# Cross-attention of a perceiver layer: keys and values by seven block products per chunk, key stacks through HBM

## The reference, cut to what matters

```python
# x (1, 256, 512), ctx_1024 (1, 25088, 512); 16 heads of 32
def _L0_xattn_ref(query, key, value, Wq, Wk, Wv, Wo):
    q = (query @ Wq.T).reshape(B, L, H, D) * scale
    k = (key @ Wk.T).reshape(B, -1, H, D)
    v = (value @ Wv.T).reshape(B, -1, H, D)
    scores = jax.nn.sigmoid(jnp.einsum('blhd,bshd->bhls', q, k))
    o = jnp.einsum('bhls,bshd->blhd', scores, v).reshape(B, L, E)
    return o @ Wo.T
x = x + _L0_xattn_ref(_layernorm(x), ctx_1024, ctx_1024, Wq, Wk, Wv, Wo)
x = x + _L0_attn_ref(_layernorm(x), ...)     # causal, 256 rows
x = x + _L0_ffn_ref(_layernorm(x), ...)      # 512 -> 2048 -> 2048 -> 2048 -> 512
```

## Time and profile before

| | |
|---|---|
| median of 3 runs | 2120.26 us (2120.01 to 2121.39) |
| span of the profiled execution | 2119.5 us |
| TensorE busy | 2096.5 us, 99% of the span |
| ScalarE busy | 1361.7 us, 64% |
| VectorE busy | 1190.9 us, 56% |
| GpSimd busy | 1022.3 us, 48% |
| DMA | 157.09 MB, mean 74 GB/s |

### The profile page before, as it was taken

The page is one execution under the profiler, slowest core; times in us unless marked ns, Lnnn a source line. Parts: engine busy times, 40 slices in busy tenths (PEclk is TensorE's granted clock), DMA queues, the critical chain, the costliest instruction groups (busy, mean ns, idle before and its releaser), DMA issues. The chain is left out here.

```text
span 2119.5 us, 42205 instructions
## 1 busy us (share of the span) xinstructions
PE 2096.5 (99%) x15810; PEld 1632.6 (77%) x15812; DVE 1190.9 (56%) x1495; ACT 1361.7 (64%) x1702; POOL 1022.3 (48%) x900
## 2 busy tenths in 40 slices
PE   9999999999999999999999999999999999988999
PEld 6777777777777777777777777777777777746998
DVE  6656556565565665656556565565655656525422
ACT  7666666666666666666666666666666666632764
POOL 5066564665646656466564665646656460000000
PEclk9999999999999999999999999999999999999999
DMA  5111211112111121111211112111121110122774
GB/s 179 42 60 40 74 45 61 58 40 74 45 61 57 40 74 45 62 57 40 74 45 63 56 40 74 45 63 56 40 74 45 63 56 21 65 101 112 277 278 168
DMA packets 43908, 157.09 MB, mean 74 GB/s; under 512 B 5600, under 2 KB 5600, under 8 KB 31200
## 3 DMA queue, kind: packets, MB, share of 16 engines
q1 hardware_dynamic: 43872, 156.59, 20.5%
HBM read 154.47 MB, written 0.52 MB: 73 GB/s over the span
## 5 line engine op out<-in xcount | busy, mean ns | idle before, releaser
L302 ACT ACTIVATE probs<-sc 128x1024 f32<-128x1024 f32 x784 | 761.6, 1022 | 371.5 <-PE sc L463 366.8
L352 DVE TENSOR_TENSOR k_stack<-kp,k_stack 32x512 fp32r<-32x512 f32 x772 | 529.5, 686 | 720.0 <-ACT k_stack L295 701.8
L295 ACT ACTIVATE k_stack<-kp 32x512 fp32r<-32x512 f32 x772 | 456.3, 591 | 257.4 <-PE kp L443 243.2
L267 POOL TENSOR_TENSOR piece_hi<-piece,zero 128x512 fp32r<-128x512 f32 x176 | 220.1, 1251 | 666.6 <-DMA piece<-w_all_dram 642.6
L463 PEld LDWEIGHTS sc<-rows_r,k_stack 96*128 96x128 f32 x3136 | 413.2, 190 | 100.0 <-issue 83.6
L463 PE MATMUL sc<-rows_r,k_stack 96*128 96x256 f32 x3136 | 460.1, 289 | 0.9 <-DMA k_stack<-k_stack 0.9
L454 PE MATMUL vp<-weights_r,c_hi 128*128 128x512 f32 x1568 | 392.9, 392 | 0.0
L443 PE MATMUL kp<-c_hi,weights_r 128*128 128x512 f32 x1544 | 386.8, 392 | 0.0
L474 PE MATMUL acc<-probs,v 128*32 128x256 f32 x6272 | 381.3, 382 | 0.1
L454 PEld LDWEIGHTS vp<-weights_r,c_hi 128*128 128x128 f32 x1568 | 282.0, 189 | 51.2 <-issue 0.8
L443 PEld LDWEIGHTS kp<-c_hi,weights_r 128*128 128x128 f32 x1544 | 277.2, 188 | 49.8
(11 more groups left out here) (135 smaller groups left out, 882.8 us busy)
## 6 DMA issues: line engine op xcount, KB each, us to landing
ctx_raw<-ctxT_dram SPq DMA_DIRECT2D x49, 1024.0 KB, 4.8
piece<-w_all_dram SPq DMA_DIRECT2D x178, 256.0 KB, 4.7
w_raw<-w_all_dram SPq DMA_DIRECT2D x44, 1024.0 KB, 4.8
weights<-wqk_dram SPq DMA_DIRECT2D x2, 1024.0 KB, 6.1
probs<-wqT_dram SPq DMA_DIRECT2D x1, 1024.0 KB, 6.0
probs<-wkT_dram SPq DMA_DIRECT2D x1, 1024.0 KB, 8.0
probs<-wvT_dram SPq DMA_DIRECT2D x1, 1024.0 KB, 11.9
k_stack<-k_stack SPq DMA_DIRECT2D x4, 256.0 KB, 3.0
```

The source lines that it names most:

```text
L267: nc.gpsimd.tensor_tensor(piece_hi[:], piece[:, t % 2, :], zero[:].to_broadcast([P, PIECE]), ALU.add).then_inc(piece_rounded, 1)
L295: nc.scalar.activation(kst[0:D, par, j, g, :], source[D * j:D * (j + 1), :], ACT.Copy).then_inc(k_hi, 1)
L302: nc.scalar.activation(probs[:, t % 2, g, :], sc[g % 2][:], ACT.Sigmoid).then_inc(probs_ready, 1)
L352: nc.vector.tensor_tensor(kst[D:2 * D, par, j, g, :], source[D * j:D * (j + 1), :], f32(kst[0:D, par, j, g, :]), ALU.subtract).then_inc(k_ ...
```

## The change

**Seven products.** The keys of a chunk are a product of a 512 by 512 weight matrix and 512 by 512 numbers of context, and so are the values. Both are now cut into 2 by 2 blocks of 256 and made by Strassen's scheme: seven block products of sums of blocks, in place of eight, with Winograd's order of the sums. A block product has 12 matmuls of 256 columns (two row halves, three terms, two steps of contraction), `k_product` and `v_product`. The seven sums of weight blocks are made once, at the start, and stay in SBUF (`wk`, `wv_c`). The seven sums of context blocks are made for each chunk (`x_combo`), hi and lo, into one set of buffers `xc`, each as soon as the value product of the chunk before it has read the old one. The products are added up in PSUM where the scheme allows it, and elsewhere by VectorE (`k_summed`, `v_summed`) or ScalarE (`k_part`, `k_first`, `v_part`, `v_first`).

**Key stacks through HBM.** A quarter of the keys (128 rows of heads by 256 context rows, two such tiles) comes out with the heads' dimensions in all 128 partitions. Its hi part and its lo part are written to a buffer in HBM (`kept`, "k_rows") and read back from there into the stack: hi rows twice, lo rows once, each time into 32 partitions. That makes 8 stores and 12 loads of 256 KB a chunk, all on SyncE's queue. The queries take the same way once.

**Two tiles weighed in one stretch.** Values are now kept for a whole chunk, twice (`v`), and `weigh` runs for tiles 0 and 1 together and for 2 and 3 together. The last chunk has no projections any more. The scan's four pieces are spread over SyncE's list.

```diff
@@ cross_attention
+        xc = sb("x_combos", [P, 7, 2, 2, HS], F32R)
...
+        kr_hi, kr_lo = sb("k_rows_hi", [P, 2, 2, HS], F32R), sb("k_rows_lo", [P, 2, 2, HS], F32R)
+        v, vt = sb("v", [P, 2, TC, E]), sb("v_part", [P, 2, HE])
@@ block.sync
+            def keep_rows(m, q):
+                at = q % 2
+                sp.wait_ge(k_hi, m * 3 + q)
+                sp.dma_start(kept[q, 0].rearrange("d r j n -> j d r n"), f32(kr_hi[:, at, :, :])).then_inc(hi_kept[q], 16)
+                sp.wait_ge(k_lo, m * 3 + q)
+                sp.dma_start(kept[q, 1].rearrange("d r j n -> j d r n"), f32(kr_lo[:, at, :, :])).then_inc(lo_kept[q], 16)
+            def stack_rows(m, q):
+                i, j = QUADRANT[q]
+                to = f32(kst[:, j, 2 * i:2 * i + 2, :, :])
+                sp.wait_ge(hi_kept[q], m * 16 + 16)
+                sp.dma_start(to[0:D], kept[q, 0]).then_inc(stacked[q], 16)
+                sp.dma_start(to[2 * D:3 * D], kept[q, 0]).then_inc(stacked[q], 16)
+                sp.wait_ge(lo_kept[q], m * 16 + 16)
+                sp.dma_start(to[D:2 * D], kept[q, 1]).then_inc(stacked[q], 16)
...
             def one(c, par, first, k_next, split_next, load_next, looped):
...
+                scan_piece(0)
+                if k_next:
+                    keep_first(m)
+                    scan_piece(1)
+                    sp.wait_ge(scores_ready, c * (TC * G) + (G + 2))
+                    stack_rows(m, 0)
+                    scan_piece(2)
+                    keep_rows(m, 1)
+                    keep_rows(m, 2)
+                    stack_rows(m, 1)
+                    keep_rows(m, 3)
+                    sp.wait_ge(scores_ready, c * (TC * G) + TC * G)
+                    stack_rows(m, 2)
+                if load_next:
+                    sp.wait_ge(x_ready, c * 7 + 14)
+                    sp.dma_start(raw[:], ctxT[c + 3]).then_inc(ctx_loaded, 16)
+                if k_next:
+                    stack_rows(m, 3)
+                scan_piece(3)
@@ block.vector
+            def x_combo(c, i):
+                if i == 1:
+                    dve.wait_ge(ctx_loaded, c * 16 + 32)
+                x_sums(c + 1, i)
+                dve.wait_ge(v_made, c * 7 + (7 + i))
+                nc.vector.tensor_copy(xc[:, i - 1, :, 0, :], x_source(raw, i)).then_inc(x_hi, 1)
+                x_rest(c + 1, i)
...
+                for i in range(1, 8):
+                    if i == 2:
+                        k_first_rest(m)
+                    elif i >= 3:
+                        k_summed(m, i)
+                        v_summed(m, 1 - par, i)
+                    if split_next:
+                        x_combo(c, i)
@@ block.tensor
+            TERMS = ((0, 0), (1, 0), (0, 1))
+            FRESH = (1, 3, 6)
+            def k_product(m, i, first=False):
...
+                elif i == 3:
+                    pe.wait_ge(k11_lo, m + 1)
+                elif i > 3:
+                    pe.wait_ge(k_sum, m * 5 + (i - 3))
+                n = 0
+                for r in range(2):
+                    for a, b in TERMS:
+                        for k in range(2):
+                            last = nc.tensor.matmul(k2[:, r, :], wk[i - 1][:, k, a, r * P:(r + 1) * P],
+                                                    xc[:, i - 1, k, b, :], start=i in FRESH and n == 0, stop=n == 11,
...
```

More of the change, by code:

```diff
@@ L309, in _, with k_part @@
[L309 to L315 removed]
+            def k_part(m):
+                act.wait_ge(k_made, m * 7 + 1)
+                nc.scalar.activation(kc[:, 0, :, :], k2, ACT.Copy).then_inc(kt_saved, 1)
@@ new lines, in v_summed @@
+            def v_summed(m, par, i):
+                add, q = SUMS[i]
+                dve.wait_ge(v_made, m * 7 + i)
+                nc.vector.tensor_tensor(v_at(par, q), vt[:] if add == "t" else v_at(par, add), v2,
+                                        ALU.add).then_inc(v_sum, 1)
+            for i in range(1, 8):
+                if i >= 3:
+                    if i == 3:
+                        dve.wait_ge(x_ready, 1)
+                    x_sums(0, i)
+                wk_rest(i)
+                x_rest(0, i)
+                if i == 2:
+                    dve.wait_ge(q_hi, 1)
+                    nc.vector.scalar_tensor_tensor(out=qr_lo, in0=sc[0][:], scalar=SCALE, in1=f32(qr_hi),
+                                                   op0=ALU.mult, op1=ALU.subtract).then_inc(q_lo, 1)
+                elif i == 4:
+                    k_first_rest(0, first=True)
+                elif i >= 5:
+                    k_summed(0, i - 2, first=True)
+                    v_summed(0, 0, i - 2)
@@ new lines, in _ @@
+            for i in (6, 7):
+                k_summed(0, i, first=True)
+                v_summed(0, 0, i)
+            def one(c, par, first, k_next, split_next, load_next, looped):
+                m = c + 1
+                if not k_next:
+                    return
+                for i in range(1, 8):
+                    if i == 2:
+                        k_first_rest(m)
[4 more added lines that the diff above has]
+                        x_combo(c, i)
@@ new lines, in v_product @@
+            def v_product(m, i, first=False):
+                if i == 1 and not first:
+                    pe.wait_ge(v_sum, m * 5)
+                elif i == 2:
+                    pe.wait_ge(vt_saved, m + 1)
+                elif i == 3:
+                    pe.wait_ge(v11_saved, m + 1)
+                elif i > 3:
+                    pe.wait_ge(v_sum, m * 5 + (i - 3))
+                n = 0
+                for r in range(2):
+                    for a, b in TERMS:
+                        for k in range(2):
+                            last = nc.tensor.matmul(v2[:, r, :], xc[:, i - 1, k, b, r * P:(r + 1) * P],
+                                                    wv_c[i - 1][:, k, a, :], start=i in FRESH and n == 0, stop=n == 11,
+                                                    skip_group_check=True)
+                            n += 1
+                last.then_inc(v_made, 1)
@@ new lines, in _, with pair, keys @@
+            for i in range(1, 8):
+                pe.wait_ge(wk_ready, i)
+                pe.wait_ge(x_ready, i)
+                k_product(0, i, first=True)
+                pe.wait_ge(wv_ready, i)
+                v_product(0, i, first=True)
+            pe.wait_ge(q_stacked, 3 * 16)
+            def one(c, par, first, k_next, split_next, load_next, looped):
+                m = c + 1
+                def pair(t, half):
+                    for g in (2 * half, 2 * half + 1):
+                        scores(c, t, g, not (first and t == 0 and half == 0))
+                def keys(i):
+                    if first:
+                        pe.wait_ge(x1c_ready, i)
+                    else:
+                        pe.wait_ge(x_ready, c * 7 + i)
+                    k_product(m, i)
+                if not k_next:
+                    pair(0, 0)
+                    pair(0, 1)
+                    pair(1, 0)
+                    for t in range(1, TC):
+                        weigh(c, par, t - 1)
+                        pair(t, 1)
+                        if t + 1 < TC:
+                            pair(t + 1, 0)
+                    weigh(c, par, TC - 1)
+                    return
+                pair(0, 0)
+                keys(1)
+                v_product(m, 1)
+                pair(0, 1)
+                keys(2)
+                v_product(m, 2)
+                pair(1, 0)
+                keys(3)
+                v_product(m, 3)
+                pair(1, 1)
+                keys(4)
+                v_product(m, 4)
+                weigh(c, par, 0)
+                weigh(c, par, 1)
+                pair(2, 0)
+                keys(5)
+                v_product(m, 5)
+                pair(2, 1)
+                keys(6)
+                v_product(m, 6)
+                pair(3, 0)
+                keys(7)
+                pair(3, 1)
+                v_product(m, 7)
+                weigh(c, par, 2)
+                weigh(c, par, 3)
```

466 lines of the change are left out of this document (259 added, 207 removed).

## The result

| | before | after |
|---|---|---|
| median of the runs (us) | 2120.82 | 2790.41 |
| lowest to highest | 2120.01 to 2122.82 | 2789.53 to 2792.29 |
| span of the profiled execution | 2119.5 | 2787.8 |
| ratio, 95% interval | | 1.316 [1.314, 1.318] |
| time per chunk | 37.84 | 51.7 |

The changed kernel is 32% slower; the forecast was 2754, with a range of 2380 to 3220.

What follows compares the result with a forecast made beforehand. TensorE bounds the kernel before; after the change the loop through four-engine stores and VectorE was to bind: start 105 + 47 chunks x 50.8 + last chunk 17.5 + rest 243.5 + 0.8 to the median = 2754 us, range 2380 to 3220.

Steps and rivals of the forecast that it cites:

- 12x + 25: SyncE's transfers before the second chunk, x being a store's cost; with landings of 3, to 88.6 us at 3.5.
- The store on four engines: Key store to HBM, 4 outermost: four engines move 64 KB each, 2.8 to 4.9 us, taken as 3.5.
- the rival in which the load binds: Four engines at 13.3 GB/s: their load, not the loop, sets 59.8 us a chunk, 3195 in all; chance 0.22.
- The loop: Third key product through VectorE's sum, stores, loads and back: 29.8 + 6x a chunk, 50.8 us at x = 3.5.
- The clock: TensorE, idle for many us in each chunk, comes back at the lower clock: some 1.7 us of work lost.
- my formula: Burst from quarter 1's first store to the chunk's load: six stores, two stacks, the load, 6x + 10.4 us.
- TensorE's own work: Products 19.9, scores 7.7, weighing 7.2, edges 0.4: 35.1 us a chunk, 2.7 less than before.
- Products and sums cost nothing by themselves: VectorE's 18.6 us a chunk hide behind TensorE's 35 as long as nothing ahead of `k_first_rest` waits.
- late VectorE: VectorE's instructions on `xc` take 1.3 times as long beside GpSimd: 1 us a chunk, 2034 us; chance 0.03.
- sixteen engines: Each store uses all sixteen DMA engines, TensorE's 35.1 us a chunk binds: 1987 us, 6% faster; chance 0.07.
- the least slack: At the third key product, waiting for `k_first_rest` some 3.2 us after scores that TensorE leaves 3.8 ahead.
- The last chunk: No projections; sigmoids 15.5, with first scores and last group some 17.5 us against 27.8; late stacks cost about the saving.

Runs made afterwards that it cites:

- e9_list: Changed kernel with stores and queries to HBM in 128-partition order, and the new chunk's context sums moved to VectorE's idle places: 2051 us.
- e3_layout: Changed kernel with only the stores' HBM buffer laid out as the 128 partitions stand, the stack loads picking the rows: 2217 us.
- e12_layout_no_scan: e3_layout with GpSimd's four operations on each weight piece cut to one column of 512: 2128 us (one run).

## Where the prediction was right and where it was wrong

**The sum.** Forecast 105 + 47 x 50.8 + 17.5 + 243.5 + 0.8. TensorE in the changed kernel, second chunk, and the last chunk's start and its first wait:

```profile
102.13 1.22 PE L703 MATMUL sc<-rows_r,k_stack_r 96*128 96x256 f32 x8
...
2514.99 1.22 PE L703 MATMUL sc<-rows_r,k_stack_r 96*128 96x256 f32 x8
2519.31 0.96 PE L703 MATMUL sc<-rows_r,k_stack_r 96*128 96x256 f32 x4 [3.10 <-DMA k_stack_r<-k_rows]
```

102.1, then 2412.9 for 47 chunks, 51.3 each, then 30.6 for the last, 242.2 and 1.7 (the last one as the profiled run's 2789.53 less its span). The start was put 2.9 too late, the loop 0.5 a chunk too short (25 us), the last chunk 13.1 too short. The terms of the start that lie outside its 12x + 25, above all the 16.1 to the end of the chunk, had no row.

**The store on four engines: right, by cause and nearly by size.** It was taken as 3.5 and is 2.7 to 3.2; the rate per engine, 83 / (0.26 x 16) = 20 and 96 / (0.27 x 16) = 22, is close to the 23.6 of the pieces and not to the 13.3 of the stack copies. So the argument that reading from few partitions slows a store did not hold for it, and the rival in which the load binds had too much weight, 0.22.

**The loop: right in its members, term by term.** Third product to the end of the fifth, clock included, 14.5 forecast and 15.7 measured; to the first store 1.2 and 2.1; burst and fixed time 33.2 and 32.6; last members 1.9 and 1.9. The clock was taken as 1.7 and is 2.5. I had misread its row: the window begins 1.6 us ahead of the first matmul, so it shows the low clock for 2.8 us behind it and not 4.4; here it lasts some 6. Burst: with a store at 3.2 my formula gives 31.4 for the 32.6, with 2.7 it gives 28.4. So a store put too high made up for something that the formula lacks, and that the term came out within 0.6 is in part luck. What is lacking has no row of its own; the formula did not have that issues took up to 3.9 us while the four engines were behind.

**TensorE's own work: near.** Products take 1.44 from start to start (fourteen are 20.2, for 19.9), two tiles 3.59 (for 3.6), and in `e9_list`, where TensorE hardly waits, it is busy 35.7 of 36.2 us a chunk, for 35.1. The products are 0.3 of the difference; the other 0.3 I cannot place.

**"Products and sums cost nothing by themselves": wrong, in two steps.** The durations came from rows of the kernel before in which each is long and reads wide; on 512 columns beside GpSimd they are not a fourth. VectorE was put at 18.6 us a chunk. It is busy 20.2 where GpSimd's work is taken away, 1.6 more, which is about what the width made wrong. It is busy 27.6 in the turn of the changed kernel and 29.5 a chunk in `e9_list`. My rival "late VectorE" took 1.3 times and 1 us a chunk; with sixteen engines a store it is 4.55 (39.65 against 35.1). The second step: I gave the least slack to the third key product. The seventh had less, and waited 2.0 a chunk (95.2 in 47) even in the changed kernel.

**The rival "sixteen engines", 1987 us:** it would have been 2217. The start is 94 against 75 (whose 40.3 had no row), and a chunk 39.65 against 35.1.

**The last chunk:** I wrote that it would wait for its late stacks by about as much as is saved, and left 17.5 in the sum. The rows show the waits (3.10 here, 3.56 later), 6.7 of the 13.1. Another 3.7 are not theirs: in `e9_list`, with no such wait, the last chunk takes 21.2 and not 17.5. The last 2.7 I did not take apart. The granted clock was 0.53 from 2519.3 to 2524.0 and from 2531.5 to 2537.0, and one weighing takes 3.38 there in place of 1.93.

## What to carry to other kernels

Read a DMA's outermost count on both sides before its bytes: with 4 there, a quarter of the engines moves it all, everything behind it on them waits, and ordering the HBM buffer like the partitions removed 573 us of the 670 lost. Then lay the list of the in-order engine beside TensorE's and put its optional work where it is idle; long stretches of TensorE that need nothing from it, like two weighings in a row, are the cover. Take its durations from rows of the same width in which its neighbour works, not from wide rows beside an idle one.

## What the runs showed of the hardware

- The number of DMA engines followed the outermost count: share 0.26 of sixteen at 4, 0.14 at 2, and two halves of a transfer, issued together, stayed at 0.14, so they ran on the same two engines.
- Four engines with rows of 1 KB, 128 partitions in all, moved 83 to 96 GB/s, 20 to 23 each; the 13.3 of the stack copies is no measure for them.
- The issue of a DMA took 0.33 us for 128 rows in order, 0.54 for a store with 4 outermost, 0.62 for a store of one block row of 32 partitions, and up to 3.9 while the four engines were behind.
- VectorE's instructions of 512 columns with two SBUF operands took, group by group, 818 to 1335 ns on average beside a working GpSimd (`e3_layout`) and 687 to 717 without it (`e12_layout_no_scan`); casts 572 to 754 and 426 to 440; with one operand in PSUM 681 and 683.
- TensorE at the lower level of its clock cost 2.5 us in a stretch of 13.2, each time it had waited 10 us.
